# A linear-attention scan, its routing and its first sends: early rows turned and two sends issued before the scan's block ends

## What is computed

```python
# linear attention, a scan over time per head (two retention factors m)
K = K * bt[..., None] + pk[:, :, None, :]
S = S * bt[..., None, None] + pk[:, :, None, :, None] * vt[:, :, None, None, :]
num = jnp.einsum('bhd,bhmdc->bhmc', pq, S)
den = jnp.einsum('bhd,bhmd->bhm', pq, K) + EPS
y = jnp.sum(num / den[..., None] * mt[..., None], axis=2)      # mt: mixing factors
...
y = jnp.moveaxis(ys, 0, 1).reshape(b, t, H) @ Wout.T + bout
z = x + y                                                       # and a layer norm of z
```

## Time and profile before

| | us |
|---|---|
| median of 3 runs | 1362.24 |
| lowest and highest run | 1358.11, 1369.48 |
| the profiled execution | 1360.32 |
| its span, first to last instruction | 1358.5 |
| DVE's last routing step in the scan block ends | 280.6 |
| first instructions of the routing block | 281.1 |
| POOL's first send, last send (start) | 284.67, 374.87 |
| SP's load of the slots (start) | 377.32 |
| first instruction of the expert block | 381.42 |

### The profile page before, as it was taken

How to read it: one execution, slowest core, us unless ns; L and a number is a source line. 1 busy time by engine, 2 the same in 40 slices (tenths; PEclk the granted TensorE clock), 3 DMA queues, 4 the chain that set the end, 5 groups by cost and what they waited for, 6 DMA issues and landing times. The chain is left out here.

```text
span 1358.5 us, 26536 instructions
## 1 busy us (share of the span) xinstructions
PE 1162.2 (86%) x7852; PEld 784.8 (58%) x7852; DVE 1043.0 (77%) x2672; ACT 888.3 (65%) x2317; POOL 858.8 (63%) x798
## 2 busy tenths in 40 slices
PE   7789999648679993896799999988969999999797
PEld 4344454335468882342577676765646777777465
DVE  6699999769859993564788788856658888887564
ACT  5534444236346560575799898977659989898663
POOL 0366656047716665315888787876568888888663
PEclk9899999769879996798999999999989999999999
DMA  4520000033212214200000000000000000000002
GB/s 134 215 67 0 1 1 1 1 88 108 65 71 71 73 55 144 67 0 24 1 2 2 2 1 2 1 1 1 0 25 2 2 2 0 1 0 2 1 1 62
DMA packets 35033, 44.08 MB, mean 32 GB/s; under 512 B 5620, under 2 KB 24977, under 8 KB 34912
## 3 DMA queue, kind: packets, MB, share of 16 engines
q1 hardware_dynamic: 30304, 34.27, 7.9%
q0 software_dynamic: 4608, 8.47, 1.9%
HBM read 22.65 MB, written 21.12 MB: 32 GB/s over the span
## 5 line engine op out<-in xcount | busy, mean ns | idle before, releaser
L2156 DVE TENSOR_TENSOR R<-bank,tab 128x1024 f32<-128x1024 f32 x128 | 155.8, 1224 | 68.9 <-ACT sq L2066 67.7
L2100 ACT ACTIVATE W<-W,nm 128x128 f32<-128x128 f32 x512 | 199.0, 396 | 0.4
L1854 POOL TENSOR_TENSOR R<-R 128x512 f32<-128x512 f32 x128 | 161.4, 1284 | 16.1 <-DVE R L2156 16.1
L2179 DVE CUSTOM_DVE_ANT_0 W<-bank,mask_q,rn 128x128 f32<-128x128 f32 x512 | 147.5, 344 | 17.3 <-PE bank L1975 13.8
L1869 POOL TENSOR_TENSOR W<-W,rden 128x512 f32<-128x512 f32 x128 | 132.6, 1042 | 40.3 <-DVE rden L2186 35.0
L1364 POOL DMA_INDIRECT expert_rows<-Yt,xin x80 | 82.4, 1030 | 67.6 <-DVE Yt L1337 48.3
L1064 POOL DMA_INDIRECT expert_slots<-tok_rows,dst x64 | 67.9, 1060 | 65.1 <-ACT tok_rows L1088 44.0
L2100 ACT ACTIVATION_READ_ACCUMULATOR W<-W,nm 128x1 f32 x512 | 99.7, 195 | 0.0
L2084 ACT ACTIVATE QK<-bank 128x512 f32<-128x512 f32 x128 | 75.3, 588 | 34.8 <-PE bank L1950 33.9
L2000 PE MATMUL bank<-PT,VA 128*64 128x128 f32 (+1 forms) x1024 | 85.4, 260 | 4.2 <-ACT PT L2108 3.3
L1975 PE MATMUL bank<-QK 64*64 64x128 f32 x2048 | 85.8, 283 | 3.4 <-DVE nm L2179 3.0
(11 more groups left out here) (358 smaller groups left out, 3506.1 us busy)
## 6 DMA issues: line engine op xcount, KB each, us to landing
expert_slots<-empty SPq DMA_DIRECT2D x8, 650.0 KB, 6.3
xin<-expert_slots SPq DMA_DIRECT2D x8, 650.0 KB
expert_rows<-empty SPq DMA_DIRECT2D x8, 512.0 KB, 6.7
pair_rows<-expert_rows SPq DMA_DIRECT2D x16, 256.0 KB, 4.2
expert_raw<-w1e_dram SPq DMA_DIRECT2D x9, 256.0 KB, 2.9
expert_raw<-w2e_dram SPq DMA_DIRECT2D x9, 256.0 KB, 3.5
tok<-x_dram SPq DMA_DIRECT2D x8, 256.0 KB, 5.2
out_dram<-tok_out SPq DMA_DIRECT2D x8, 256.0 KB, 2.7
```

The source lines that it names most:

```text
L1854: nc.gpsimd.tensor_tensor(halves[:, :, 0, :, z, :], halves[:, :, 0, :, z, :], halves[:, :, 1, :, 1 - z, :], ALU.add).then_inc(summed, 1)
L2100: m = nc.scalar.activation(x, x, ACT.Exp, scale=-1.0, bias=nm[:, p % RING, j:j + 1], accum_out=den[:, p % RING, j:j + 1])
L2156: nc.vector.tensor_tensor(R[:, i, qk, :, :].rearrange("p c (h d) -> p c h d", d=DH), x, y.to_broadcast([P, 2, HEADS, DH]), ALU.mult).then_ ...
L2179: m = nc.vector.tensor_tensor_reduce(W[:, p % RING, j * P:(j + 1) * P], ps[BS[i]][:, cols], k.const["mask_q"][:, cols], rn[:, par, 2 * s + ...
```

## The change

The early tiles' rows are turned and stored, and their first two sends issued, in the scan block.

- **One buffer.** `k.rows` (5120 columns, `token_rows`) lives through both blocks and the experts: it first holds `mix0` and two chunks of `mix1` (the rest is in `mix_rest`), then the token rows and the fallback mask `WE`, then the experts' pair rows `Y`. The last scan step must have read the factors (`mixed_r`) before rows are written. The fallback sum is now formed in its bank, without `Z`.
- **Routing of the early tiles.** `router(5)`, its copy, `route_shift`, the `Exp` and `route_chances` stand in the last round; the two `route_top` stand around `term(7, 7)`; the eight experts are split in `expert_start` and `expert_end`, with steps of the last chunk's norm between. `route_places` no longer computes shares: they are computed between experts, and `k.dst` of the first choice signals `placed`.
- **PE and ACT.** PE's last rounds are written out: `count_early` and six `turn_rows` alternate with `summed(7)`, `z_variance`, `x_centre` and `x_variance` of the last chunk; ACT's `keep_rows` likewise.
- **POOL.** After the scan's work it writes the two extra columns for 24 tiles, waits for `placed`, and issues two sends; the other 22 early first-choice sends open the routing block.
- **The routing block.** PE turns 8 tiles, ACT copies two banks, DVE's splits of `H` come ahead of the logits.

```diff
+ROW = P + 2
+FIRST_SENDS = 2
...
+def share_sum(dve, x, step):
+
+    step(dve.tensor_tensor(x.sm, x.p1, x.p2, ALU.add))
+    step(dve.tensor_scalar(x.sm, x.sm, 1e-9, None, ALU.max))
...
+def share_out(k, dve, x, n, n0, step):
+
+    tiles = slice(n0, n0 + n)
+    step(dve.reciprocal(x.rs, x.sm))
+    dve.tensor_tensor(k.share[:, 0, tiles], x.p1, x.rs, ALU.mult)
+    return dve.tensor_tensor(k.share[:, 1, tiles], x.p2, x.rs, ALU.mult)
+
...
+def send_row(k, c, n):
+    k.nc.gpsimd.indirect_dma_start(k.xs[:, :], bass.IndirectOffsetOnAxis(ap=k.dst[:, c, n:n + 1], axis=0),
+                                   k.tok[:, n, :], None, bounds_check=NE * CAP - 1,
+                                   oob_is_err=False).then_inc(k.sent[c][n // 8], 16)
...
-        step(dve.scalar_tensor_tensor(k.dst[:, c, tiles], x.fb, float(NE * CAP), x.slot, ALU.mult, ALU.add))
+        dve.scalar_tensor_tensor(k.dst[:, c, tiles], x.fb, float(NE * CAP), x.slot, ALU.mult, ALU.add).then_inc(placed, 1)
+        dve.wait_ge(placed, c + 1)
...
+        def mix(m, c):
+            at = m * T + c * CH
+            split = NPB * 2 * CH
+            return k.rows[:, at:at + CH] if at < split else mix_rest[:, at - split:at - split + CH]
...
+                def turn_rows(q):
+                    if q == 0:
+                        pe.wait_ge(t_done, NS * NCH)
+                        pe.wait_ge(normed2, EARLY // 4)
+                    if q >= 4:
+                        pe.wait_ge(tok_sb, q - 3)
+                    for n in range(4 * q, 4 * q + 4):
+                        t = nc.tensor.transpose(ps[BV + q % 4][:, (n % 4) * P:(n % 4 + 1) * P], k.H[:, n * P:(n + 1) * P],
+                                                k.const["ident"][:])
+                    t.then_inc(turned, 1)
...
+                    if c == EARLY // 4 + 1:
+                        router(c - 2)
...
-                pe.wait_ge(rot, 2 * NCH)
-                for e in range(NE):
-                    count_early(e)
+                c = NCH - 1
+                summed(c, 6)
+                count_early(0)
+                summed(c, 7)
+                turn_rows(0)
+                count_early(1)
+                z_variance(c)
+                count_early(2)
+                turn_rows(1)
+                count_early(3)
+                turn_rows(2)
+                count_early(4)
+                x_centre(c)
+                count_early(5)
+                turn_rows(3)
+                x_variance(c)
+                count_early(6)
+                turn_rows(4)
+                count_early(7)
+                turn_rows(5)
...
+                def keep_rows(q):
+                    if q == 0:
+                        act.wait_ge(mixed_r, 2 * NCH)
+                    act.wait_ge(turned, q + 1)
+                    nc.scalar.activation(k.tok[:, 4 * q:4 * q + 4, 0:P], ps[BV + q % 4][:].rearrange("p (a b) -> p a b", a=4),
+                                         ACT.Copy).then_inc(tok_sb, 1)
...
+                    if c == EARLY // 4 + 1:
+                        keep_logits(c - 2)
...
+                    if c == EARLY // 4 + 1:
+                        act.wait_ge(shifted, 1)
+                        nc.scalar.activation(x.pr, x.pr, ACT.Exp).then_inc(exped, 1)
...
+                c = NCH - 1
+                z_square(c)
+                keep_rows(0)
+                root(c, var1, logged1, rstd1, rs1)
+                keep_rows(1)
+                keep_rows(2)
+                x_square(c)
+                keep_rows(3)
+                root(c, var2, logged2, rstd2, rs2)
+                keep_rows(4)
+                keep_rows(5)
 
...
+                c = NCH - 1
+                route_top_value(k, nc.vector, x, EARLY, 0, step, x.p1)
+                term(c, 7)
+                route_top_place(k, nc.vector, x, EARLY, 0, step, x.oh1)
+                step(nc.vector.scalar_tensor_tensor(x.pr, x.oh1, -2.0, x.pr, ALU.mult, ALU.add))
+                route_top_value(k, nc.vector, x, EARLY, 0, step, x.p2)
+                route_top_place(k, nc.vector, x, EARLY, 0, step, x.oh2)
+                step(nc.vector.tensor_tensor(x.oh, x.oh1, x.oh2, ALU.add))
+                expert_start(0)
+                residual(c)
+                expert_end(0)
+                expert_start(1)
+                x_scale(c - 1)
+                expert_end(1)
+                expert_start(2)
+                share_sum(nc.vector, x, step)
+                expert_end(2)
+                expert_start(3)
+                share_out(k, nc.vector, x, EARLY, 0, step).then_inc(share_set, 1)
+                expert_end(3)
+                expert_start(4)
+                z_scale(c)
+                x_add(c)
+                expert_end(4)
+                for e in range(5, NE):
+                    expert_start(e)
+                    expert_end(e)
+                route_places(k, nc.vector, x, EARLY, 0, ps[BKS], step, placed)
+                x_scale(c)
 
             @block.gpsimd
             def _(pool):
@@ -868,7 +988,7 @@
 
                 def weigh(c, m):
                     pool.wait_ge(phi, 2 * c + 2)
...
+                pool.wait_ge(share_set, 1)
+                pool.wait_ge(mixed_r, 2 * NCH)
+                nc.gpsimd.tensor_copy(k.tok[:, 0:EARLY, P:P + 1].rearrange("p n o -> p (n o)"),
+                                      k.share[:, 0, 0:EARLY]).then_inc(tails, 1)
+                nc.gpsimd.tensor_copy(k.tok[:, 0:EARLY, P + 1:P + 2].rearrange("p n o -> p (n o)").bitcast(mybir.dt.uint32),
+                                      k.const["tokid"][:, 0, 0:EARLY]).then_inc(tails, 1)
+                pool.wait_ge(tails, 2)
+                pool.wait_ge(k.cleared, 16 * N_CLEAR)
+                pool.wait_ge(tok_sb, 1)
+                pool.wait_ge(placed, 1)
+                for n in range(FIRST_SENDS):
+                    send_row(k, 0, n)
...
-            for n in range(NT):
+            for n in range(EARLY, NT):
...
-            for q in range(NCH):
-                rows(q)
-                if q % 2:
-                    rounded(q // 2)
             split_high(0)
             split_high(1)
+            for q in range(EARLY // 4, NCH):
+                rows(q)
+            rounded(0)
+            rounded(1)
             act.wait_ge(shifted, 1)
             nc.scalar.activation(pr[:], pr[:], ACT.Exp).then_inc(exped, 1)
+            rounded(2)
+            rounded(3)
             nc.scalar.preload_act_table(ACT.Gelu)
...
-            dve.wait_ge(k.late_in, 16 * N_LATE)
-            for q in range(EARLY // 8):
-                first_tail(q)
             V.memset(before[:, 0:1], 0.0)
+            split_low(0)
+            split_low(1)
+            dve.wait_ge(logit_mm, 1)
+            route_shift(V, x, LATE, step, shifted)
             piece_low(0)
             piece_low(1)
-            dve.wait_ge(logit_mm, 1)
-            route_shift(V, x, LATE, step, shifted)
-            split_low(0)
-            split_low(1)
             dve.wait_ge(exped, 1)
...
-                    V.scalar_tensor_tensor(Z[:], outer(c)[:], w["b2e"][:, NE:NX], WE[:],
+                    V.scalar_tensor_tensor(outer(c)[:], outer(c)[:], w["b2e"][:, NE:NX], WE,
                                            ALU.add, ALU.mult).then_inc(z_r, 1)
                     dve.wait_ge(z_r, c + 1)
-                    V.tensor_tensor(k.XT[:, chunk(c)], k.XT[:, chunk(c)], Z[:], ALU.add).then_inc(added, 1)
+                    V.tensor_tensor(k.XT[:, chunk(c)], outer(c)[:], k.XT[:, chunk(c)], ALU.add).then_inc(added, 1)
...
+            k.rows = k.sb("token_rows", [P, NPB * 2 * CH], ctx=keep)
+            k.tok = k.rows[:, 0:NT * ROW].rearrange("p (n w) -> p n w", w=ROW)
```

More of the change, by code:

```diff
@@ L772, in x_scale, with expert_start, expert_end @@
                     nc.vector.tensor_tensor(k.H[:, chunk(c)], ps[BK][:], rs2[:], ALU.mult).then_inc(normed2, 1)
[L774 to L775 removed]
+                def expert_start(e):
+                    eligible(nc, x, e, EARLY, k.taken[:, e, :], elig_r)
+                def expert_end(e):
+                    over(nc, x, e, EARLY, ps[BKS], step, counted)
+                for c in range(-1, NCH):
+                    last, now, more = 0 < c, 0 <= c, c + 1 < NCH
                     if last:
```

136 lines of the change are left out of this document (62 added, 74 removed).

## The result

The changed kernel took 1353.14 us (median of 7 runs, 1348.01 to 1355.88), the kernel before 1362.24 (also a median of 7 runs, 1358.11 to 1369.48). The ratio is **0.9925, with a 95% interval of 0.9901 to 0.9948**: faster by 9 us, within 1%, as forecast (1354, 1347 to 1363). Two more comparisons of the same pair, on two other chips, gave 0.9949 (0.9922 to 0.9976) and 0.9964 (0.9927 to 1.0000).

A forecast was written before the change was run, and what follows sets the result against it. POOL's chain of sends was taken to set the routing block's end, so its start counts: +0 for the first round, -7.1 for the chain, 0 beyond, 1360.3 to 1353.2; with half the median's 1.9 offset, 1354, range 1347 to 1363.

The forecast's parts named there:

- third send: POOL's first send behind the barrier: at about 281.1 against 288.15, 9.0 or 5.0 us earlier, middle 7.1.
- `residual`: Last chunk's norm, after the last sum: 259.8 or 260.8, some 3 to 4 us later; sign 259.5 to 261.
- Last scan round: Three groups of routing steps move among the terms, mostly covered by waits for PE: 0.2 us later, ending about 254.5.
- The added wait: PE idles 2.4 us ahead of the first count; the last sum behind it takes 1.0 us, or probably 2.0.
- Places: DVE's slots for the first choice, after the eighth expert: 273.8 at full clock or 277.8 at half clock.
- The two sends: POOL's two early sends ahead of the barrier: 3.2 us together (1.56, 0.30, 1.31).
- Barrier and restart: POOL, last at the scan block's barrier, releases it in 0.5 us; the third send needs 0.6 more.
- Routing block: DVE ends about 365.5, POOL's last send 368.7, 3 us to spare; DVE's shorter part is worth nothing by itself.
- Behind it: After the sends: same load, landing and barrier, so 0 us added and every stage as long as before.
- full overlap: PE stays at 2.4 GHz, POOL's start behind the barrier is short: gain 9 to 10 us, 1351; chance 0.22.
- the blocked sends: Early sends beside DVE's places wait for the end of `x_scale`: 1.9 later, gain 5.2 at best, 1356; chance 0.10.
- The slower line: PE's order serialises norm and DVE's routing in the scan tail: third send 289.9, 1.7 later, 1362; chance 0.05.

The follow-up runs named there:

- e2_six_early_sends: Changed kernel with six sends instead of two ahead of the barrier; 1351.32 us, ratio 0.9913 to the kernel before.
- e3_sum_first: Changed kernel with the last output sum ahead of the first count in PE's order; 1352.45 us, ratio 0.9925 to the kernel before.
- after_again: Changed kernel itself, unedited, on chip 14, one of the slow kind; 1395.86 us (1387.49 to 1398.21).
- e10_rows_in_routing_block_again: Changed kernel with turns and copies of 24 early tiles back in the routing block, no early sends, chip 7; 1395.23 us, ratio 0.9960 to the kernel before.

## Why the prediction was right, step by step

**The sum held, with three errors that nearly cancel.** Forecast: third send at 281.1, 27.3 us behind the start of a last term at 253.8. Measured: 26.85 behind T in the profiled execution. Places came 1.1 sooner than said and the two sends took 0.7 less, barrier and restart took 1.4 more. The path was the one forecast; that the total came out within 0.5 us is in part luck. Of the signs that the prediction names, the end of the last term (255.15, said within 0.5 of 254.3) and `residual` (261.30, said 259.5 to 261) lie just outside, both by the later T; the others came, but for the 0.9 us of the last item below.

- *Last scan round.* Said +0.2, measured +0.1: from the first term cited in the earlier trace rows to the last it is 10.09 us now and was 9.98. T itself is 0.85 later, which lies inside its wandering.
- *The added wait.* PE idle 2.50 (said 2.4), count and sum, residual 6.84 behind T, between the 6.0 and 7.0 that the two values given are from 253.8. In six of eight executions with this PE order and the turns in place the last sum took the full clock, 5.9 behind T. "Probably at 1.2 GHz" was right for the profiled one and wrong for most.
- *Places.* Said: first choice placed at 273.8 or 277.8, middle 275.8, or 22.0 behind T. Measured 20.9 (275.32), and 19.7 to 20.0 where the last sum ran fast. An expert's turn cost 1.24 to 1.36 among the first four (said 1.20); the half-clock end was too dark, since the clock was up from 262 to 268, but not for the second variance. The prediction also misread the kernel before: it says that five of eight turns came after the norm's last big matmul, and all eight counts did, the first at 267.22, as the second variance came to its end. Five came after the last scaling (270.35).
- *The two sends.* Said 3.2, measured 2.5 (1.19 + 0.30 + 0.99).
- *Barrier and restart.* Said 0.5 + 0.6, measured 1.8 + 0.7. **This is the term that failed**: its price was read from a barrier that DVE released, and this one is released by a send that has to land.
- *Routing block.* DVE's last add ends at 365.43 (said 365.5), POOL's last send ends at 369.13 (said 368.7), SP's load stands 1.5 behind it. "Worth nothing by itself" held, but the spare time is 9 us and not 3, as e2_six_early_sends showed.
- *Behind it.* 6.7 us at the slots' load have become 5.9 at the final stores; 0.9 us were lost in code that the change does not touch, which lies inside the wandering of that stretch.

Of the rivals, full overlap named part of the truth (the clock), not its time; the blocked sends did not come: the first started at 276.33, before `x_scale` did, and took 1.19 us, the second, with DVE idle, 0.99; six in a row took 1.19 and then 0.97 or 0.98. (That rival's "5.2 at best" is its gain from the middle; from the better end it would be 9.0 - 1.9 = 7.1.) The Trainium skill, SBUF — State Buffer ("SBUF: two separate sides"), gives 3.1 us for such a DMA beside a DVE `tensor_copy`, and has DVE instructions in a 2-port mode as its condition. Only the first of the two sends lay beside DVE steps (a cast and `x_scale`), and no run shows in which mode these ran, so the rule is not tested here. In the routing block, where DVE was busy 73 of 85 us, the longest of the changed kernel's sends took 1.50. The slower line did not come either: waits of 2.29 and 1.88 are the two places where PE's order did serialise; no other count made DVE wait for more than 0.71.

## What to carry to other kernels

Before moving a DMA ahead of a barrier, price its landing: two sends moved in front cost 1.8 us of waiting at the block's end, by the times for the second to land, and were worth some 0.3 us net, while the same engine's barrier without them took 0.3 to 0.5. Count from a fixed event just ahead of the change, not from the span's start: T wandered by up to 3.5 us between executions, more than most single steps here are worth. Small TensorE work that is placed in the waits of a serial chain can pay twice, by leaving the critical path and, in part of the stretch here, by keeping the granted clock up.

## What the runs showed that was not expected

**A block's end waits behind a POOL send, by the times until it has landed.** 1.8, 1.7 and 2.0 us from the end of the last send to PE's first instruction behind the barrier (changed kernel, e3_sum_first, e2_six_early_sends), and 1.7 to 1.8 in the six other kernels with two early sends and nothing behind them; 0.3 where there was no send, 0.5 where 1.94 us of other POOL work stood behind it.

**On two of the chips, engines other than POOL stalled while the sends ran.** DVE of after_again:

```profile
297.52 0.17 DVE L212 SCALAR_TENSOR_TENSOR cols<-bank,elig 128x8 f32<-128x8 f32 x1 [3.63 <-remote]
...
305.27 0.17 DVE L212 SCALAR_TENSOR_TENSOR cols<-bank,elig 128x8 f32<-128x8 f32 x1 [6.37 <-remote]
...
314.41 0.17 DVE L212 SCALAR_TENSOR_TENSOR cols<-bank,elig 128x8 f32<-128x8 f32 x1 [7.68 <-remote]
```

PE's count for the second of these had ended at 299.2, DVE went on at 305.27. The word "remote" stands where the profile finds no releaser on this core. The windows from 285 to 370, of the changed kernel's first profile and of after_again (DVE is the third busy time, POOL the fifth):

```profile
285.00:370.00 85.00, 59.54 (x252) 37.79 (x252) 73.27 (x170) 40.53 (x65) 64.06 (x67) 0.90 0.30 95
```

```profile
285.00:370.00 85.00, 34.94 (x101) 21.72 (x102) 28.48 (x94) 14.66 (x25) 59.56 (x66) 0.54 0.23 71
```

DVE was busy 73.3 us and now 28.5, while POOL's sends kept their pace of 1.28 us; behind the last send the steps ran at their usual distance. DVE's last add ended at 411.8 instead of 365.4 and PE's first expert turn came 37.5 us later, which is most of the 43 us between the two spans. The kernel before was not profiled on these chips; that its 40 us have the same cause is not shown. Without twelve of the sends DVE's last add came 13.2 and 17.1 us earlier, where the sends ended 15.7 and 16.3 us earlier. What delays the signals stays open, and so does why e10_rows_in_routing_block_again got through it 4.5 us earlier than the changed kernel although its sends ended 5.4 us later.
